# Two-layer transformer block on one core: the last sequence routed in two groups of two tiles, three weight pieces of the first expert loaded earlier

## What is computed

```python
x = x + ga * (o.reshape(b, t, VAL_DIM) @ Wo)              # output projection
h = _layernorm(x) * (1 + cb) + sb                         # cb, sb per sequence
logits = rms_normed(h) * F ** -0.5 * router_scale @ router_logits      # 8 experts
_, choices = approx_max_k(logits, k=2)                    # two experts a token
gate_out = ragged_dot(sorted_rows, w_gate)                # 512 -> 2 x 512, per expert
activation = gelu(gate_out[:, 0]) * gate_out[:, 1]
out = ragged_dot(activation, linear) * per_expert_scale   # 512 -> 512
x = x + gb * (sum over the two choices of combine_weight * out)
```

## Time and profile before

| what | value |
|---|---|
| time before, median of 3 runs | 2610.04 us (2605.77 to 2614.66) |
| the profiled execution's own time | 2621.22 us |
| its span | 2619.5 us |
| PE busy over the span | 2362.1 us (90%) |
| DVE, POOL, ACT busy | 1606.0 (61%), 1256.7 (48%), 1139.9 us (44%) |
| mean granted clock of PE | 0.949 |

### The profile page before, as it was taken

How to read it: one execution, slowest core, us unless ns; L and a number is a source line. 1 busy time by engine, 2 the same in 40 slices (tenths; PEclk the granted TensorE clock), 3 DMA queues, 4 the chain that set the end, 5 groups by cost and what they waited for, 6 DMA issues and landing times. The chain is left out here.

```text
span 2619.5 us, 34297 instructions
## 1 busy us (share of the span) xinstructions
PE 2362.1 (90%) x9812; PEld 1595.7 (61%) x9812; DVE 1606.0 (61%) x2464; ACT 1139.9 (44%) x2390; POOL 1256.7 (48%) x1189
## 2 busy tenths in 40 slices
PE   7999979999999998797999994779899867999999
PEld 6788855555555554684888882535445325788877
DVE  4240239999999997585222223689999986411253
ACT  2333029999999997223222223732323113311121
POOL 1022036666666663566645322279998984111110
PEclk9999989999999998888999996889999997999999
DMA  5245435555555653776434315544444446101021
GB/s 181 77 141 183 121 100 156 173 174 162 167 165 167 174 166 128 210 219 224 138 120 154 110 51 157 194 166 166 174 163 175 171 144 181 65 25 48 16 89 65
DMA packets 264547, 370.58 MB, mean 141 GB/s; under 512 B 33528, under 2 KB 116488, under 8 KB 264432
## 3 DMA queue, kind: packets, MB, share of 16 engines
q1 hardware_dynamic: 228496, 301.25, 36.8%
q0 software_dynamic: 11040, 36.64, 4.2%
q10 hardware_dynamic: 24896, 31.24, 3.4%
HBM read 255.09 MB, written 113.98 MB: 141 GB/s over the span
## 5 line engine op out<-in xcount | busy, mean ns | idle before, releaser
L1082 ACT ACTIVATE attn_probs<-attn_ps_score,attn_nmax 128x512 f32<-128x512 f32 x512 | 342.8, 674 | 2.2 <-DVE attn_nmax L1156 2.2
L2713 PE MATMUL scan_ps_o<-scan_qs,scan_sel 128*128 128x512 f32 x512 | 279.5, 637 | 65.1 <-DVE scan_qs L2654 58.5
L2671 DVE TENSOR_TENSOR_SCAN scan_st<-scan_ps_dec,scan_kv 128x512 f32<-128x512 f32 x256 | 305.8, 1209 | 11.5 <-POOL scan_kv L2620 11.5
L989 PE MATMUL attn_ps_score<-attn_KK,attn_X 64*128 64x512 f32 x512 | 215.0, 467 | 20.8 <-ACT attn_probs L1082 20.4
L1170 DVE SCALAR_TENSOR_TENSOR attn_mixed<-attn_probs,attn_cf,attn_mixed 128x512 f32<-128x512 f32 x256 | 193.3, 755 | 9.1
L2713 PEld LDWEIGHTS scan_ps_o<-scan_qs,scan_sel 128*128 128x128 f32 x512 | 90.4, 195 | 167.5 <-DVE scan_qs L2654 105.0
L2620 POOL TENSOR_TENSOR scan_kv<-gla_vb,gla_gk 128x512 f32<-128x512 f32 x128 | 161.1, 1288 | 36.7 <-POOLq L2139 30.5
L1145 DVE TENSOR_REDUCE attn_raw<-attn_ps_score 128x2 f32<-128x1024 f32 x128 | 156.4, 1222 | 29.0 <-PE attn_ps_score L989 28.0
L989 PE MATMUL attn_ps_score<-attn_KL,attn_X 64*128 64x512 f32 x512 | 172.7, 422 | 0.0
L989 PE MATMUL attn_ps_score<-attn_KK,attn_Y 64*128 64x512 f32 x512 | 160.0, 398 | 0.8 <-POOL attn_Y L879 0.8
L2620 POOL TENSOR_TENSOR scan_kv<-gla_vb,scan_gk 128x512 f32<-128x512 f32 x128 | 159.6, 1284 | 2.4 <-DVE scan_st L2671 2.4
(11 more groups left out here) (559 smaller groups left out, 6451.7 us busy)
## 6 DMA issues: line engine op xcount, KB each, us to landing
gla_vb<-gv SPq DMA_DIRECT2D x256, 256.0 KB
rows_x<-attn_zeros SPq DMA_DIRECT2D x32, 1024.0 KB, 13.5
late<-rows SPq DMA_DIRECT2D x32, 384.0 KB, 9.1
attn_spread<-rows SPq DMA_DIRECT2D x32, 384.0 KB, 9.0
moe_raw<-in_L_ffn_gating POOLq DMA_DIRECT2D x6, 2048.0 KB, 9.5
moe_xb<-rows_x SPq DMA_DIRECT2D x39, 256.0 KB, 2.7
rows_y<-moe_y ACTq DMA_DIRECT2D x39, 256.0 KB, 2.0
sg<-proj_tile SPq DMA_DIRECT2D x32, 256.0 KB, 2.0
```

The source lines that it names most:

```text
L989: last = nc.tensor.matmul(ps_score[n][:, j, :], weights, y[p][half, :], start=(r == 0), stop=(r == len(terms) - 1))
L1082: nc.scalar.activation(probs[b][:, at_j, :], ps_score[n][:, j, :], ACT.Exp, bias=nmax[b][:, at_j:at_j + 1], accum_out=Z[b][:, at_j:at_j + ...
L2671: V.tensor_tensor_scan(st[r][:, :], ps_dec[n % 2][:, :], kv[r][:, :], 0.0, ALU.mult, ALU.add).then_inc(st_ready, 1)
L2713: nc.tensor.matmul(ps_o[w][:, :], sel[:, P - GPH - GPH * d:2 * P - GPH - GPH * d], qs[i % RING][:, :], start=(d == 0), stop=(d == HALF - 1 ...
```

## The change

- **Groups.** The routing steps take a group in place of a sequence: groups 0 to 2 are sequences 0 to 2, group 3 is tiles 12 and 13, group 4 tiles 14 and 15. `norm`, `turn`, `take`, `logits`, `choice`, `count`, `places`, `shift` and `squares` run per group.
- **Where they stand.** PE: `turn(2)` and `count(1)` move from behind tile 13 to behind tile 12, `logits(2)` from 14 to 13, `count(2)` into tile 14, `turn(3)` behind tile 14, `logits(3)` into tile 15; behind the last tile stand `count(3)`, `modulation(0)`, `turn(4)`, `logits(4)`, `modulation(1)`, `count(4)`. DVE: `places(1)` before the gating of tile 13, `norm(3)` behind tile 13, `choice(2)` and `places(2)` before tile 14, `choice(3)` before tile 15; the multiplication of the last two tiles moves from POOL to DVE (`scale_last`). ACT takes its steps to match, and `squares(3)`, `squares(4)` stand behind `modulation(1)`.
- **Scatters.** POOL scatters tiles 12 and 13 in the output projection; two tiles instead of four are left for the expert stage.
- **Weights.** A buffer `raw0` of three pieces is kept through both stages. SP loads the first three `gating` pieces of expert 0 into it at tile 10 of the output projection. In the expert stage three pieces are left to load. DVE makes all six low parts before the tables instead of behind them, and ACT the six high parts before the square root and the exponential. The second expert's first three pieces don't wait for `w_lo` any more.

```diff
+        GROUPS = [(b, 0, TT) for b in range(B - 1)] + [(B - 1, 0, TT // 2), (B - 1, TT // 2, TT)]
...
+                if n == 2 * TT + 2:
+                    gating = a["L0_ffn_gating"].rearrange("e (c p) n -> e p c n", p=P)
+                    for k in range(EARLY):
+                        sp.dma_start(s["raw0"][:, k, :], gating[0, :, k, :]).then_inc(s["raw0_in"][k], 16)
...
-                for n in range(NT - SCATTER_BEHIND, NT - TT - 2):
+                for n in range(NT - SCATTER_BEHIND, 2 * TT):
                     scatter(n)
                 scale(B - 1)
-                for n in range(NT - TT - 2, NT - TT):
+                for n in range(2 * TT, NT - TT // 2):
                     scatter(n)
...
+            TURN_AT = {TT + 1: 0, 2 * TT + 1: 1, 3 * TT: 2, NT - 2: 3}
+            LOGITS_AT = {TT + 2: 0, 2 * TT + 2: 1, 3 * TT + 1: 2}
+            COUNT_AT = {2 * TT + 1: 0, 3 * TT: 1}
...
-                    if h is not None and n == NT - 1 and c == KC // 2:
+                    if n == NT - 2 and c == KC // 2 + 1:
                         count(B - 2)
+                    if n == NT - 1 and c == KC // 2:
+                        logits(B - 1)
...
-            if h is not None:
-                for k in two:
-                    modulation(k)
-            turn(B - 1)
-            if h is not None:
-                logits(B - 1)
-                count(B - 1)
+            count(B - 1)
+            modulation(0)
+            turn(LAST)
+            logits(LAST)
+            modulation(1)
+            count(LAST)
...
-            after(B - 1)
-            if h is not None:
-                choice(B - 1)
-                places(B - 1)
+            places(B - 1)
+            shift(B - 1)
+            scale_last()
+            shift(LAST)
+            choice(LAST)
+            places(LAST)
...
+EARLY = 3
...
-            for n in range(NT - TT, NT):
+            for n in range(NT - TT // 2, NT):
                 scatter_rows(nc, s, n)
...
-                        pool.wait_ge(raw_in[k], 32)
+                        pool.wait_ge(raw_in[k], 16 if k < EARLY else 32)
...
+            for k in range(CHUNKS):
+                low_weights(k)
+
             V.tensor_scalar(ms[:, :], s["ssq"][:, :], 1.0 / D, 1e-6, ALU.mult, ALU.add).then_inc(std_in, 1)
...
-            for k in range(CHUNKS):
-                low_weights(k)
             for u in range(AHEAD):
                 low_rows(u)
```

More of the change, by code:

```diff
@@ L1616, in places, with scale_last @@
-            def places(b):
-                tiles = slice(TT * b, TT * (b + 1))
-                counts = lambda k: ps_logit[:, (1 + k) * TT * E:(2 + k) * TT * E].rearrange("p (n e) -> p n e", e=E)
+            def scale_last():
+                b, t0, t1 = GROUPS[LAST]
+                dve.wait_ge(hn_ready, LAST + 1)
+                dve.wait_ge(rows_in[b % 2], 16 * (b // 2 + 1))
+                for t in range(t0, t1):
+                    V.tensor_tensor(h[:, b * TT + t, :], hn[b % 2][:, t, :], rows[b % 2][:, 1, :], ALU.mult).then_inc(scaled, 1)
@@ new lines, in _, with choice @@
+            rc = Chain(dve, route_step)
+            def choice(g):
+                tiles, many = slots_of(g), len(tiles_of(g))
+                lg = s["logit"][:, tiles, :]
+                pi = lg.unsqueeze(3).to_broadcast([P, many, E, E])
+                pj = lg.unsqueeze(2).to_broadcast([P, many, E, E])
+                wins, even, first = (z[:, 0:many, :, :] for z in (beats, ties, below))
+                order = rank[:, 0:many, :]
+                if g == 0:
+                    dve.wait_ge(route_const, N_ROUTE)
+                dve.wait_ge(logit_taken, g + 1)
+                rc.step(V.tensor_tensor(wins, pj, pi, ALU.is_gt))
+                rc.link(V.tensor_tensor(even, pj, pi, ALU.is_equal))
+                rc.link(V.tensor_tensor(even, even, first, ALU.mult))
+                rc.link(V.tensor_tensor(wins, wins, even, ALU.add))
+                rc.link(V.tensor_reduce(order, wins, AX.X, ALU.add))
+                V.tensor_scalar(s["chosen"][:, tiles, :], order, 2.0, None, ALU.is_lt).then_inc(chosen_ready, 1)
+                rc.step(V.tensor_scalar(s["first_e"][:, tiles, :], order, 0.0, None, ALU.is_equal))
+                rc.link(V.tensor_scalar(s["second_e"][:, tiles, :], order, 1.0, None, ALU.is_equal))
@@ L1620, in places @@
+            def places(g):
+                tiles, many = slots_of(g), len(tiles_of(g))
+                counts = lambda k: ps_logit[:, (1 + k) * TT * E:(1 + k) * TT * E + many * E].rearrange("p (n e) -> p n e", e=E)
                 base = s["base"]
-                dve.wait_ge(count_done, b + 1)
-                for t in range(TT):
-                    n = TT * b + t
+                at, mine = place[:, 0:many, :], pick[:, 0:many, :]
+                dve.wait_ge(count_done, g + 1)
+                for t, n in enumerate(tiles_of(g)):
@@ L1640, in _ @@
                     dve.wait_ge(x_in[p], 32 * (b // 2 + 1))
-                if h is not None and n == NT - 1:
+                if n == 3 * TT + 1:
+                    places(1)
+                if n == NT - 2:
                     choice(B - 2)
                     places(B - 2)
+                if n == NT - 1:
+                    choice(B - 1)
                 dve.wait_ge(mm_done, n + 1)
@@ L1769, in load_weights @@
             def load_weights(e):
[L1770 to L1771 removed]
+                for k in range(CHUNKS) if e else range(EARLY, CHUNKS):
+                    if e and k >= EARLY:
                         sp.wait_ge(w_lo, k + 1)
```

248 lines of the change are left out of this document (119 added, 129 removed).

## The result

| what | before | after |
|---|---|---|
| time, median | 2611.32 us (6 runs, 2605.77 to 2615.84) | 2623.49 us (6 runs, 2619.98 to 2631.83) |
| ratio after / before | | 1.0047, 95% interval 1.0031 to 1.0062 |
| profiled execution, span | 2621.22, 2619.5 us | 2619.98, 2618.3 us |

The change costs 12.2 us (8.1 to 16.2), where 5.2 were forecast. The profiled execution of after is the fastest of its six, that of before is slower than any of the six beside it, and has the lower granted clock (0.949 against 0.953). So the two traces are compared from one event on, the end of `chosen` of `choice(1)`, which is 1164.35 before and 1154.86 after.

The account below looks back on a forecast made before the run. PE is always busy in the expert blocks, so the first `gate` matmul's start decides. Barrier 4.0, DVE's order 2.0, clock 0.4, block-2 wait -1.2: +5.2 us on the median 2610.04, so 2615.2; range 2605 to 2624.

Parts of the forecast that it names:

- the forecast's own case: Whole kernel: the main forecast without any rival, +5.2 us or 2615.2, bounds 2607 to 2623; chance 0.60.
- rival C: Expert stage: the last weight piece lands late, `gate` comes 11 us later, total +14 or 2624 us; chance 0.18.
- the case of slower by over 0.3%: Whole kernel: slower by more than 0.3% (7.8 us), chance 0.29; within 0.3% had 0.63, faster 0.08.
- Waits behind tile 12: Output projection, PE: waits 1.3 us before `turn(2)` for normed rows and 4.0 us before `count(1)` for `chosen_ready`.
- Rival A: Output projection: DVE's multiply of `choice(1)` slips between POOL's operations, shortening the wait; total -0.9 or 2609 us; chance 0.12.
- PE to the end of tile 15: Output projection: PE's queued work and clock losses end tile 15 at 1192.0, 7.9 us later than before.
- The clock terms: Output projection: lower granted clock after PE's waits adds 2.4 us at tile 13 and 1.7 at tile 14.
- The tail: From the end of tile 15 to the barrier: 18.0 us in place of 22.0, ending with ACT's squares.
- the middle term: The term for PE to the end of tile 15: +7.9 us, set against the tail's 18.0 in place of 22.0.
- Scatters worth nothing: Behind the barrier: rows come 5.1 us earlier, but DVE's list keeps `gate` at 21.7 at best, no gain.
- DVE's order behind the barrier: Expert stage: tables now wait for the last remaining weight piece; +2.0 us, between -0.1 and +3.5.
- Around `gate`: Expert stage, PE: +0.4 us for low clock at the first matmuls, -1.2 for a hidden wait at block 2.

Follow-up runs that it names:

- tables_first: The changed kernel with DVE's tables and ACT's root and exponential back ahead of the weights' low and high parts, early pieces kept; ratio to before 1.0018.
- weights_only: The kernel before plus the three early weight pieces and the new DVE and ACT order behind the barrier, without the groups; ratio to before 1.0011.
- The halves: The two runs weights_only and routing_only, each with one half of the change; 2.9 and 5.5 us above before.
- by_need: The changed kernel with DVE's list behind the barrier ordered by when results are needed, root and weights of the sum last, ACT to match; ratio to before 1.0058.
- routing_only: The changed kernel without the early weight pieces and with the tables ahead of the low parts, groups and fewer scatters kept; ratio to before 1.0021.
- all_three: The changed kernel with by_need's list, squares ahead on ACT, and modulation(0) in PE's wait behind tile 12; ratio to before 1.0053.
- deferred: all_three with the rest of DVE's tables moved into the expert loop, two operations behind each block from block 2; ratio to before 1.0001.
- deferred_inside: deferred with PE's routing steps moved inside or behind tiles 13 to 15 and places(2) behind tile 14's gating; ratio to before 1.0006.
- three_behind: deferred_inside with tile 13's two scatters moved behind the barrier, six there instead of four; ratio to before 1.0018.
- turn_inside: The changed kernel with turn(2) inside tile 13, count(1) behind it, logits(2) inside tile 14 and count(2) near its end; ratio to before 1.0044.
- squares_first: The changed kernel with ACT's squares(3) ahead of router(4) and squares(4) ahead of modulation(1); ratio to before 1.0060.
- modulation_early: The changed kernel with modulation(0) in PE's wait behind tile 12 and modulation(1) in modulation(0)'s old place; ratio to before 1.0033.
- before_deferred: weights_only with DVE's list behind the barrier by need and the rest of the tables in the expert loop; ratio to before 1.0017.

## Why the prediction was right and wrong

The range held the time by 0.5 us (2623.5 below 2624), and the sign was right. That it did is partly luck: the forecast's own case ended at 2623, and the edge of 2624 came from rival C, which did not happen. The size was not: the time lies in the case of slower by over 0.3%, which had 0.29, and not in that of 0.63.

- **Waits behind tile 12: right.** 1.3 and 4.0 forecast, 1.22 and 3.77 measured. Rival A did not happen: DVE's multiply took 2.46 us again, and `chosen` ended at the same distance from the end of tile 12 within 0.3. In all profiles of after's order the multiply had POOL beside it; none shows the other case.
- **PE to the end of tile 15: +7.9 forecast, +9.0 measured.** The clock terms held in size: tile 13 lost 1.75 (2.4 forecast), tile 14 with its count 1.9 (1.7). In one point the mechanism was off: tile 13 did not start at the low level but at 1.00, and fell 0.8 us later. Missed was a wait of 1.30 of `logits(3)`: I had counted its work inside tile 15 and not its input, the `hT` that ACT began 2.1 us after PE's last row of `turn(3)` was issued. For that start, too, the profile names no releaser.
- **The tail: 18.0 forecast, 19.9 measured.** Its chain was as described, up to the squares. One term was mis-sized: `modulation(1)`, taken at 3.5 (half of 7.03), took 5.25. With the middle term, +7.9 and -4.0 became +9.0 and -2.1: +6.9 at the barrier in place of +4.0. That the modulation and the squares were the only chain was too simple: with the squares ahead no more than 0.8 is gained, and DVE's places, behind ACT's late copy, are next.
- **Scatters worth nothing: wrong by 1.6 us, and without effect.** I put the best case of DVE's order at 21.7; tables_first shows 20.1. My 1.2 us until the first high part is there holds only with the low parts first.
- **DVE's order behind the barrier: +2.0 forecast, +3.9 measured.** This is the term that failed most. I had the price of a landing as late as before (3.5) and took less, because half of the scatter traffic is gone. weights_only refutes that: with eight scatters DVE waits 3.94 us for its pieces, with four 4.09. The last piece was cast 10.1 us behind the barrier (9.4 taken for the bound). Rival C, which needed 11, did not happen; what happened lies just short of it.
- **Around `gate`: -0.8 forecast, -1.0 measured.** The first 24 matmuls took 6.7 us, not more than before; the wait for block 2 kept 0.86 of 1.48.

Sum of the trace at `gate(1)`: 6.9 + 3.9 - 1.0 = 9.8 us, forecast 5.2. Of the missing 4.6, 1.9 are the order, 1.8 the modulation, 1.3 the wait of `logits(3)`, less smaller terms. The measured 12.2 contains 9.8 in its interval; the 2.4 between them are not explained. The halves, 2.9 and 5.5, sum to 8.4, which is the same within their intervals. In the traces they don't add: at `gate(1)` the halves are 1.1 and 3.1 us behind before, and after is 9.8. About 2 us of that are the order, which costs 3.8 us with the routing of before and 5.5 with the groups, since it also hides what fewer scatters bring; the rest lies between `gate` and `gate(1)`, where the halves alone gain 1.6 and 2.3 us and after only 1.0, and in the spread of single traces.

## What to carry to other kernels

When a list of one engine is reordered, ask of each entry what it waits for and who waits behind it: an entry that waits on a DMA belongs behind those that wait for nothing (5.5 us here), and an entry that nobody needs soon must leave the stretch, not only move back in it (by_need gained 7.6 us at `gate` and lost 10.1 one step later). Splitting the last group of a pipeline shortens its tail, but the steps move onto the busy engine ahead of the tail: here 2 us came off the tail and 9 were added before it. Where two forecasts of a landing differ, take the row before the argument about traffic: the third of the pieces loaded behind the barrier was cast at 9.4 us in before and at 9.4 in routing_only, with half the scatters; only the last two came sooner there.

## What the runs showed of the hardware that was not expected

- **A barrier behind scatters.** In all fourteen profiles the barrier came 0.26 to 0.28 us behind the last work of DVE or ACT, except in three, where it came 3.55, 3.57 and 3.57 us behind POOL's last indirect DMA, with all others done for at least 1.5 us (all_three, deferred, deferred_inside). In none did it come less than 3.5 behind such a DMA. In three_behind, with that DMA 5.9 us before, the barrier followed DVE by 0.28 again.
- **A late copy.** In eight of the fourteen profiles ACT copied the last logits 1.7 to 5.3 us behind the end that the profile gives for PE's rows of them. In after, turn_inside, squares_first, modulation_early and by_need ACT was idle for 5.7 to 5.8 us before it copied the last logits, in routing_only and tables_first for 7.3, in three_behind for 3.0, and the profile names no releaser. In the five with 5.7 to 5.8 the idle time is nearly the same whether the copy came 2.6 or 5.3 us behind PE's rows, so it seems to hang on what ACT did before and not on PE; that is not shown. In all_three, deferred and deferred_inside, where the modulation was early and the squares ahead, and in the three kernels with the routing of before, the copy followed within 0.1 us of PE's last row. Since three_behind has the same order on ACT and PE as deferred_inside, the order is not all of it. The cause stays open, and so does what it costs the tail.
- **Landing of the weight pieces.** The last of three pieces was cast 9.7 to 10.5 us behind the barrier in all twelve profiles with the early load, with four scatters beside it (after 10.06), six (three_behind 9.87) or eight (weights_only 9.90, before_deferred 9.73); of six pieces it was 14.5 with four scatters (routing_only) and 16.9 with eight.
- **DVE beside POOL.** 25 small table operations took 7.3 us with POOL idle and 21.4 beside its splitting (by_need). Stretched were products and sums of two tiles, up to 2.33 us in place of 0.29; the reductions kept their 0.29.
